# A graph network in one kernel: the third attention's row products in two halves around the turned scan, and residual biases added during the passes

## The chip, the cores and the metric

The kernel runs on one core of one Trainium2 chip, as one program. The metric is the device time of that core in microseconds (us), the median of three runs. The engines are TensorE (PE; its weight loads are PEld), VectorE (DVE), ScalarE (ACT), GpSimd (POOL) and SyncE (SP), which only issues transfers.

## The reference, cut to what matters

There are N = 5000 nodes with 128 features and E = 85000 edges sorted by their target `dst` (the last 5000 in the list before sorting are self loops). Four layers, each `x = x + layer(relu(layernorm(x)))`:

```python
# 0: mean over the incoming edges, then a product
x = x + segment_sum(h[src], dst) / (deg + 1e-6) @ W.T + b
# 1: an edge MLP, its mean, a product, relu
e = relu(concat(h[src], h[dst]) @ W_edge.T)
x = x + relu((segment_sum(e, dst) / deg) @ W_node.T + b_node)
# 2: two graph attentions (16 heads of 8) with elu between them
x = x + gat(elu(gat(h, W1, a_src1, a_dst1) + b1), W2, a_src2, a_dst2) + b2
# 3: dot-product attention (2 heads of 64)
alpha = (q[dst] * k[src]).sum(-1) / 8
a = exp(alpha - segment_max(alpha, dst)[dst])
x = x + segment_sum(a * v[src], dst) / segment_sum(a, dst) + (h @ Wskip + bskip)
```

## The kernel before

**Layout.** X, acc, nodeQ and their like hold all nodes in SBUF: 128 nodes on the partitions, 40 blocks of them along the free axis. The edges are cut into 704 steps of up to 128 edges that all point into one block; eight steps are a group, and there are 88 groups (NG). For each step there are one-hot matrices O (edge to node) and Ot (turned), made in the first pass and kept in DRAM as bf16.

**Stages.** The program is a row of blocks, each with one instruction stream per engine and all engines meeting between blocks: preparation; `norm_phase`; `sum_pass` (layer 0); `sum_to_mlp`; `mlp_pass` (layer 1); `mlp_to_gat`; `softmax_pass("gat")`; `gat_to_gat`; `softmax_pass("gat")`; `gat_to_dot`; `softmax_pass("dot")`, which is called the third attention here; `dot_to_out`.

**A pass** runs one turn per group. GpSimd issues eight indirect gathers a turn (L1000), which bring the rows of the source nodes into GT, a ring of four groups; a place in the ring is free again when VectorE has made the group's values (L1427). SP loads the one-hots (`load_hots`). ScalarE casts them to f32 (L1016 makes Ot32 of the turned ones, two groups deep; L1237 makes O). An order written out by hand sets what each engine does in a turn, with groups that are one or two ahead or behind in it. In the third attention:

- TensorE: the maxima of group p (L1313), the weighted sums of p-2 into psA (L1334), the turning of the logits of p+1 (L1297), the maxima for each edge of p (L1321), the turning back of the scanned maxima of p+1 (L1303, `pe_segT`, into psT), and last the products that bring the query rows of the target nodes to the edges of p+2 (`pe_toedge`, which calls `rows_to_edges`, L1023, eight of 128x128 f32 into psD). A product of f32 is two MATMUL instructions in the trace, so a group of eight is x16. The block numbers come from registers: `loaded` loads eight of them from a table before the products, and eight others (the places of the sums) at the head of the turn.
- VectorE: the product of psD with the keys and its sum over each head for p+1 (L1346, L1355), the running maxima of p (L1378 to L1413), the addition of the sums of p-2 to acc (L1436, L1440), the scan of the turned logits of p+1 (L1362), the difference to the maximum for p (L1418, L1421), three small steps on the turned back maxima of p+1 (`dve_lastmax`, L1370 to L1374), and the values of p (`dve_values`, L1427).
- ScalarE: among others, clearing the places in psA (L1269), and exp of the differences (L1275, the factor that L1427 needs; L1278).

All waits are on semaphores that count groups. One product waits for `turned32` (the cast) and for `prodded` of the group before (psD has been read).

**The stages between the passes** work on 20 units of two blocks, each engine again with an order by hand in which units at several lags alternate (`units`). VectorE's bias additions stand there: L645 in `sum_to_mlp`, L843 (`plus_row`) in `gat_to_gat` and `gat_to_dot`, L928 in `gat_to_dot`; each is followed by an addition to X, a minimum or the like. L862 is one step of elu in `gat_to_gat`. The finished rows of a table are stored by SP (`store_rows`, L525), unit by unit. `dot_to_out` has VectorE divide and add for 20 units (L791 to L980), and when all are done SP stores X in two transfers (L985, L986).

Of the kernel before, what the change touches and what calls it, by code (L numbers as in the profile page):

```python
# [65 lines left out]
def program(nc, x, src, dst, w0, b0, w_edge, w_node, b_node, w1, as1, ad1, b1, w2, as2, ad2, b2,  # L66
# [28 lines left out]
    with ctx:  # L95
# [119 lines left out]
        out_sem = sem("out_stored")  # L215

# [415 lines left out]
        def sum_to_mlp(table):  # L632

            with nc.Block() as block:
                @block.vector
                def _(eng):
                    for unit in units(8):
# [5 lines left out]
                        if n := unit(3):  # L643
                            eng.wait_ge(*made(n.u))
                            eng.tensor_tensor(n.Y, n.ps[:, :, 0:D], bias_row(0), ALU.add).then_inc(biased.sem, 1)  # L645
                            eng.wait_ge(*biased(n.u))
                            eng.tensor_tensor(n.at(X), n.at(X), n.Y, ALU.add).then_inc(xnew.sem, 1)
# [46 lines left out]
            close((degrees, own, denom, mean, cleared, flip, lhs, made, biased, xnew, *norm_counts, flip2, lhs2, made2, kept,  # L694
# [150 lines left out]
        def gat_to_gat(table):  # L845

            with nc.Block() as block:
                @block.vector
                def _(eng):
                    self_shares_1(eng)  # L850
                    self_shares_2(eng)
                    for unit in units(8):
# [7 lines left out]
                        if n := unit(4):  # L860
                            eng.wait_ge(*powered(n.u))
                            eng.tensor_scalar(n.Y2, n.Y2, -1.0, None, ALU.add).then_inc(skipped.sem, 1)  # L862
                            eng.wait_ge(*skipped(n.u))
                            eng.scalar_tensor_tensor(out=n.Y, in0=n.Y, scalar=0.0, in1=n.Y2, op0=ALU.max,
                                                     op1=ALU.add).then_inc(normed.sem, 1)
# [32 lines left out]
            close((own, denom, mean, biased, lowered, powered, skipped, normed, *gat_counts), UNITS)  # L898
            close_stored()

        def gat_to_dot(table):

            with nc.Block() as block:
                @block.vector
                def _(eng):
                    self_shares_1(eng)
                    self_shares_2(eng)
                    for unit in units(8):
                        if n := unit(0):
                            slot_free(eng, n, skipped)  # L910
                            self_and_sums(eng, n)
                            plus_row(eng, n, 3)
                            eng.wait_ge(*biased(n.u))
# [10 lines left out]
                        if n := unit(8):  # L924
# [3 lines left out]
                            eng.tensor_tensor(n.Y, n.ps[:, :, D:2 * D], bias_row(7), ALU.add).then_inc(powered.sem, 1)  # L928
                            eng.wait_ge(*powered(n.u))
                            eng.tensor_tensor(n.at(X), n.at(X), n.Y, ALU.add).then_inc(skipped.sem, 1)  # L930
# [16 lines left out]
                def _(eng):  # L947
                    for unit in units(8):
                        if n := unit(4):
                            slot_free(eng, n, powered)  # L950
                            eng.wait_ge(*normed(n.u))
                            flip_y(eng, n, flip2)
# [8 lines left out]
                def _(eng):  # L961
# [4 lines left out]
            close((own, denom, mean, biased, xnew, cleared, *norm_counts, flip2, lhs2, made2, kept, made3, lowered,  # L966
                   powered, skipped), UNITS)
            close_stored()

        def dot_to_out():  # L970

            with nc.Block() as block:
                @block.vector
                def _(eng):
                    for u in range(UNITS):
                        n = Unit(u)
                        slot_free(eng, n, xnew)
# [5 lines left out]
                def _(eng):  # L983
                    eng.wait_ge(*xnew(UNITS - 1))
                    eng.dma_start(out[0:FULL * P, :].rearrange("(b p) f -> p b f", p=P), X[:, 0:FULL, :]).then_inc(out_sem, 16)  # L985
                    eng.dma_start(out[FULL * P:N, :], X[0:REST, FULL, :]).then_inc(out_sem, 16)  # L986
                    eng.wait_ge(out_sem, 32)
# [30 lines left out]
        def rows_to_edges(eng, p, b):  # L1018

            eng.wait_ge(*turned32(p.g))  # L1020
            eng.wait_ge(*prodded(p.g - 1))
            for j in range(G):
                ins = eng.matmul(psD[:, j, :], Ot32[:, p.q, j, :], at_block(nodeQ, b[j], D), start=True, stop=True)  # L1023
            ins.then_inc(toedge.sem, 1)

        def load_hots(eng, p, rows_free, turned_free):
# [6 lines left out]
            for c in turned_free:  # L1033
# [3 lines left out]
               .then_inc(ring_hotT[p.k].sem, 16)  # L1037

# [18 lines left out]
        def sum_pass(table):  # L1057

            w = D + 1
            with nc.Block() as block:  # L1060
# [37 lines left out]
                def _(eng):  # L1098
                    tables_stored(eng)
# [104 lines left out]
        def softmax_pass(kind, table, h):  # L1204
# [76 lines left out]
            def pe_toedge(eng, p):  # L1281
                if not gat:
                    rows_to_edges(eng, p, loaded(eng, "blocks", blk, p.g, G, NB - 1))
                    return
# [157 lines left out]
            with nc.Block() as block:  # L1442
# [37 lines left out]
                def _(eng):  # L1480
                    def turn(p):
                        if p.has(-2):
                            off = pe_places(eng, p.plus(-2))
# [99 lines left out]
```

## Time and profile before

| | |
|---|---|
| median of 3 runs | 5167.67 us (5164.42 to 5171.92) |
| the profiled execution, its own time | 5178.65 us |
| its span, first to last instruction | 5176.9 us |
| mean granted TensorE clock | 0.686 |
| busy: PE, PEld, DVE | 3180.1, 2813.0, 2733.0 us |
| busy: ACT, POOL | 2152.4, 3365.2 us |

The trace is of the profiled execution. A row of busy time sums an engine's instructions; "idle before" is the time that the engine stood still ahead of an instruction and, behind the arrow, what released it ("issue": nothing that the profile shows, such as loading registers). Matmuls are pipelined, so the time of a group of them includes waiting for the first to come through.

### The profile page before, as it was taken

The page shows a single profiled execution, that of the slowest core. Times are in us where ns is not written, and L with a number is a line of the kernel's source. Part 1 is how long each engine was busy: PE and PEld are TensorE (multiplying, and loading weights), DVE is VectorE, ACT ScalarE, POOL GpSimd, SP SyncE. Part 2 cuts the span into 40 slices and gives each one's busy share as a digit, 9 for nine tenths or more (in the row PEclk, how much of TensorE's full clock was granted, in tenths as well). Part 3 has the DMA queues.
Part 4 walks back from the last instruction along what each step waited for, and adds up shares of the span by engine and source line. Part 5 has one row for each costly group of instructions (what it writes and reads, how often), then busy time and mean ns, then how long its engine had stood idle before and what let it go on. Part 6 is the DMA issues. An engine that isn't in the chain of part 4 may idle for free. (4 is left out here: it accounts for less than half of the span.)

```text
span 5176.9 us, 111400 instructions
## 1 busy us (share of the span) xinstructions
PE 3180.1 (61%) x29524; PEld 2813.0 (54%) x29525; DVE 2733.0 (53%) x6724; ACT 2152.4 (42%) x6586; POOL 3365.2 (65%) x3551
## 2 busy tenths in 40 slices
PE   1555555566666665666666646666665566666664
PEld 0444444455655654565656536566564466666664
DVE  4222222332222225677777767777777666666666
ACT  2222222243333325666666556666664333333332
POOL 1777777557777772777777537777773366666662
PEclk9766666687777777656666656665666777676766
DMA  4333333233333332444444224444441344444442
GB/s 125 106 105 105 105 105 104 80 101 105 105 105 105 105 97 60 115 117 118 117 113 117 78 83 118 117 113 118 117 117 54 111 141 134 133 132 135 134 133 74
DMA packets 331553, 563.97 MB, mean 109 GB/s; under 512 B 79101, under 2 KB 149773, under 8 KB 331438
## 3 DMA queue, kind: packets, MB, share of 16 engines
q0 software_dynamic: 124288, 289.37, 21.2%
q1 hardware_dynamic: 207170, 273.48, 16.3%
q8 instruction: 42, 0.69, 0.1%
q14 instruction: 53, 0.43, 0.0%
HBM read 490.38 MB, written 72.84 MB: 109 GB/s over the span
## 5 line engine op out<-in xcount | busy, mean ns | idle before, releaser
L1000 POOL DMA_INDIRECT GT<-table,srcI x3520 | 3351.0, 952 | 1688.0 <-issue 1055.0
L1334 PE MATMUL psA<-V,O 128*128 128x144 f32 (+1 forms) x4224 | 932.8, 403 | 17.4 <-ACT psA L1269 14.9
L1334 PEld LDWEIGHTS psA<-V,O 128*128 128x128 f32 x4224 | 864.8, 294 | 24.0 <-issue 18.7
L1023 PE MATMUL psD<-nodeQ,Ot 128*128 x2816 | 608.0, 403 | 386.9 <-ACT Ot L1016 298.8
L1023 PEld LDWEIGHTS psD<-nodeQ,Ot 128*128 128x128 f32 x2816 | 561.6, 305 | 416.0 <-issue 416.0
L1055 DVE TENSOR_TENSOR acc<-acc,psA 128x1032 f32 (+1 forms) x176 | 215.1, 1222 | 703.6 <-PE psA L1134 673.9
L1269 ACT COPY psA<-consts 128x1296 f32<-128x1296 f32 (+1 forms) x264 | 318.6, 1207 | 368.0 <-DVE acc L1440 368.0
L1180 DVE TENSOR_TENSOR prod<-psD,GT 128x1024 f32<-128x1024 f32 x88 | 107.7, 1224 | 667.1 <-DMA GT<-table,srcI 667.1
L1046 PE MATMUL psA<-zerob 1*128 1x258 bf16 (+1 forms) x704 | 164.5, 378 | 414.1 <-issue 329.1
L1258 ACT COPY nodeM<-newM 128x16 f32 x1408 | 307.7, 219 | 259.2 <-ACT nodeM L1258 230.3
L1440 DVE TENSOR_TENSOR acc<-acc,psA 128x1296 f32 (+1 forms) x264 | 385.6, 1461 | 55.4 <-PE psA L1334 26.2
L1303 PE MATMUL psT<-ident,seg 128*128 128x128 f32 (+1 forms) x264 | 95.7, 362 | 470.1 <-DVE seg L1362 470.1
L1010 ACT COPY srcI<-srcT 128x8 int32 (+1 forms) x440 | 84.3, 193 | 689.3 <-DMA GT<-table,srcI 682.1
L1263 ACT ACTIVATE resc<-diff 128x16 f32<-128x16 f32 (+1 forms) x264 | 55.9, 212 | 733.5 <-DVE acc L1436 687.6
L1165 ACT ACTIVATE V<-prod 128x1024 f32<-128x1024 f32 x88 | 93.0, 1057 | 616.4 <-DVE prod L1180 616.4
L1321 PEld LDWEIGHTS psS<-newM,Ot 128*128 128x128 bf16 x6336 | 189.3, 99 | 290.8 <-DVE newM L1413 288.9
L1321 PE MATMUL psS<-newM,Ot 128*128 128x16 bf16 (+1 forms) x6336 | 211.3, 174 | 212.8 <-DVE newM L1413 212.5
L1134 PE MATMUL psA<-GT,O 128*128 128x129 f32 x1408 | 329.8, 427 | 0.0
L1134 PEld LDWEIGHTS psA<-GT,O 128*128 128x128 f32 x1408 | 305.9, 329 | 36.6 <-issue 36.6
L1046 PEld LDWEIGHTS psA<-zerob 1*128 1x128 bf16 x704 | 68.7, 118 | 470.5 <-issue 447.6
L1427 DVE TENSOR_TENSOR V<-GT,psA 128x1024 f32<-128x1024 f32 x264 | 320.8, 1215 | 3.7 <-ACT psA L1275 3.4
L1303 PEld LDWEIGHTS psT<-ident,seg 128*128 128x128 f32 (+1 forms) x264 | 43.4, 164 | 492.1 <-DVE seg L1362 323.0
(221 smaller groups left out, 5304.1 us busy)
## 6 DMA issues: line engine op xcount, KB each, us to landing
Ob<-onehots SPq DMA_DIRECT2D x352, 256.0 KB
Ot<-onehots_turned SPq DMA_DIRECT2D x352, 256.0 KB
GT<-table,srcI POOLq DMA_INDIRECT x3520
onehots<-Ob SPq DMA_DIRECT2D x88, 256.0 KB
onehots_turned<-Ot SPq DMA_DIRECT2D x88, 256.0 KB
first<-first_dram SPq DMA_DIRECT2D x176, 64.0 KB
first_dram<-GT SPq DMA_DIRECT2D x18, 384.0 KB, 5.1
table<-GT SPq DMA_DIRECT2D x40, 144.0 KB, 1.9
```

Of the source, the lines that this page charges most:

```text
L1000: eng.indirect_dma_start(out=GT[:, p.k, j, 0:table.shape[1]], out_offset=None, in_=table, in_offset=bass.IndirectOffsetOnAxis(ap=srcI[:, p ...
L1023: ins = eng.matmul(psD[:, j, :], Ot32[:, p.q, j, :], at_block(nodeQ, b[j], D), start=True, stop=True)
L1046: eng.matmul(psA[:, a:a + 2, 0:w], zerob[0:1, 0:P], zerob[0:1, 0:2 * w], start=True, stop=False, skip_group_check=True)
L1055: eng.tensor_tensor(a, a, psA[:, :, 0:w], ALU.add).then_inc(added.sem, 1)
L1134: ins = eng.matmul(to, O[:, p.q, j, :], GT[:, p.k, j, 0:w], start=False, stop=j == G - 1, skip_group_check=True)
L1258: eng.copy(at_block(nodeM, b[j], h), by_step(newM[:, p.q, 0:HG])[:, :, j]).then_inc(noted.sem, 1)
L1269: eng.copy(places, consts[:, 0:1, :].unsqueeze(1).to_broadcast([P, 3, 3, VW])).then_inc(emptied.sem, 1)
L1303: eng.transpose(segR, seg[0:HG, p.q, :], ident[0:HG, 0:HG]).then_inc(segT.sem, 1)
L1321: ins = eng.matmul(edge_max[:, j, :], Ot[:, p.k, j, :], part, start=n == 0, stop=n == 2)
L1334: ins = eng.matmul(flatA[:, bass.ds(off[j], VW)], O[:, p.q, j, :], V[:, p.q, j, 0:VW], start=False, stop=j == G - 1, skip_group_check=True)
L1427: eng.tensor_tensor(v[:, :, :, 0:C], heads(GT[:, p.k, :, f0:f0 + D], h), wide(factors, C), ALU.mult)\
L1440: eng.tensor_tensor(to, to, places, ALU.add).then_inc(added.sem, 1)
```

## The change

Four edits:

- In the third attention TensorE issues the products L1023 as two halves of four, one ahead of the turning back (L1303) and one behind it, and loads their block numbers at the head of the turn. On VectorE `dve_lastmax` moves behind `dve_values`. The attentions of layer 2 keep their order.
- Three biases (b of layer 0, b2, bskip) are added to all of X by `add_to_x`, in four instructions of ten blocks each, at the head of the first sum, the second attention and the third attention, ahead of VectorE's wait for the stored table. L645, L843 in `gat_to_dot`, and L928 go, and the additions to X read psA or its like directly.
- elu's two steps (L862, L864) become one.
- `dot_to_out` stores each unit's rows as soon as they are done, 21 transfers in place of 2.

```diff
--- before
+++ after
@@ -213,6 +213,7 @@
         out_sem = sem("out_stored")
+        leaned = Count(sem("leaned"), 4)
@@ -641,10 +642,9 @@
                         if n := unit(3):
+                            eng.wait_ge(leaned.sem, leaned.base)
                             eng.wait_ge(*made(n.u))
-                            eng.tensor_tensor(n.Y, n.ps[:, :, 0:D], bias_row(0), ALU.add).then_inc(biased.sem, 1)
-                            eng.wait_ge(*biased(n.u))
-                            eng.tensor_tensor(n.at(X), n.at(X), n.Y, ALU.add).then_inc(xnew.sem, 1)
+                            eng.tensor_tensor(n.at(X), n.ps[:, :, 0:D], n.at(X), ALU.add).then_inc(xnew.sem, 1)
                         if n := unit(3):
@@ -859,10 +859,8 @@
                             eng.wait_ge(*powered(n.u))
-                            eng.tensor_scalar(n.Y2, n.Y2, -1.0, None, ALU.add).then_inc(skipped.sem, 1)
-                            eng.wait_ge(*skipped(n.u))
-                            eng.scalar_tensor_tensor(out=n.Y, in0=n.Y, scalar=0.0, in1=n.Y2, op0=ALU.max,
-                                                     op1=ALU.add).then_inc(normed.sem, 1)
+                            eng.scalar_tensor_tensor(out=n.Y, in0=n.Y2, scalar=-1.0, in1=n.Y, op0=ALU.add,
+                                                     op1=ALU.max).then_inc(normed.sem, 1)
                         if n := unit(8):
@@ -907,10 +905,10 @@
                         if n := unit(0):
-                            slot_free(eng, n, skipped)
+                            slot_free(eng, n, flip2)
                             self_and_sums(eng, n)
-                            plus_row(eng, n, 3)
-                            eng.wait_ge(*biased(n.u))
+                            eng.wait_ge(leaned.sem, leaned.base)
+                            eng.wait_ge(*mean(n.u))
                             eng.tensor_tensor(n.at(X), n.at(X), n.Y, ALU.add).then_inc(xnew.sem, 1)
@@ -925,9 +923,7 @@
                                                      op0=ALU.mult, op1=ALU.add).then_inc(lowered.sem, 1)
-                            eng.tensor_tensor(n.Y, n.ps[:, :, D:2 * D], bias_row(7), ALU.add).then_inc(powered.sem, 1)
-                            eng.wait_ge(*powered(n.u))
-                            eng.tensor_tensor(n.at(X), n.at(X), n.Y, ALU.add).then_inc(skipped.sem, 1)
+                            eng.tensor_tensor(n.at(X), n.ps[:, :, D:2 * D], n.at(X), ALU.add).then_inc(skipped.sem, 1)
@@ -947,7 +943,8 @@
                         if n := unit(4):
-                            slot_free(eng, n, powered)
+                            slot_free(eng, n, lowered)
+                            slot_free(eng, n, skipped)
                             eng.wait_ge(*normed(n.u))
@@ -974,6 +970,8 @@
                         n = Unit(u)
+                        if not u:
+                            eng.wait_ge(leaned.sem, leaned.base)
                         slot_free(eng, n, xnew)
@@ -981,10 +979,14 @@
                 def _(eng):
+                    whole_rows = out[0:FULL * P, :].rearrange("(b p) f -> p b f", p=P)
+                    for u in range(UNITS - 1):
+                        eng.wait_ge(*xnew(u))
+                        eng.dma_start(whole_rows[:, u * H:(u + 1) * H, :], X[:, u * H:(u + 1) * H, :]).then_inc(out_sem, 16)
                     eng.wait_ge(*xnew(UNITS - 1))
-                    eng.dma_start(out[0:FULL * P, :].rearrange("(b p) f -> p b f", p=P), X[:, 0:FULL, :]).then_inc(out_sem, 16)
+                    eng.dma_start(whole_rows[:, (UNITS - 1) * H:FULL, :], X[:, (UNITS - 1) * H:FULL, :]).then_inc(out_sem, 16)
                     eng.dma_start(out[FULL * P:N, :], X[0:REST, FULL, :]).then_inc(out_sem, 16)
-                    eng.wait_ge(out_sem, 32)
+                    eng.wait_ge(out_sem, 16 * (UNITS + 1))
             close((own, denom, mean, xnew), UNITS)
@@ -1015,13 +1017,15 @@
-        def rows_to_edges(eng, p, b):
-            eng.wait_ge(*turned32(p.g))
-            eng.wait_ge(*prodded(p.g - 1))
-            for j in range(G):
+        def rows_to_edges(eng, p, b, half=None):
+            if not half:
+                eng.wait_ge(*turned32(p.g))
+                eng.wait_ge(*prodded(p.g - 1))
+            for j in range(G) if half is None else range(half * G // 2, (half + 1) * G // 2):
                 ins = eng.matmul(psD[:, j, :], Ot32[:, p.q, j, :], at_block(nodeQ, b[j], D), start=True, stop=True)
-            ins.then_inc(toedge.sem, 1)
+            if half != 0:
+                ins.then_inc(toedge.sem, 1)
@@ -1035,6 +1039,13 @@
                .then_inc(ring_hotT[p.k].sem, 16)
+        def add_to_x(eng, c):
+            for q in range(4):
+                part = X[:, q * NB // 4:(q + 1) * NB // 4, :]
+                eng.tensor_tensor(part, part, bias[:, c:c + 1, :].to_broadcast([P, NB // 4, D]), ALU.add).then_inc(leaned.sem, 1)
+            leaned.close(1)
@@ -1096,6 +1107,7 @@
                 def _(eng):
+                    add_to_x(eng, 0)
                     tables_stored(eng)
@@ -1201,7 +1213,7 @@
-        def softmax_pass(kind, table, h):
+        def softmax_pass(kind, table, h, to_x=None):
             gat = kind == "gat"
@@ -1279,9 +1291,6 @@
             def pe_toedge(eng, p):
-                if not gat:
-                    rows_to_edges(eng, p, loaded(eng, "blocks", blk, p.g, G, NB - 1))
-                    return
                 eng.wait_ge(*staged(p.g))
@@ -1481,6 +1490,8 @@
                             off = pe_places(eng, p.plus(-2))
+                        if not gat and p.has(2):
+                            b = loaded(eng, "blocks", blk, p.g + 2, G, NB - 1)
                         if p.has(0):
@@ -1489,14 +1500,21 @@
                             pe_maxedge(eng, p)
+                        if not gat and p.has(2):
+                            rows_to_edges(eng, p.plus(2), b, 0)
                         if p.has(1):
...
                         if p.has(2):
-                            pe_toedge(eng, p.plus(2))
+                            if gat:
+                                pe_toedge(eng, p.plus(2))
+                            else:
+                                rows_to_edges(eng, p.plus(2), b, 1)
                     sweep(eng, NG, turn, early=2, late=2)
...
                 def _(eng):
+                    if to_x is not None:
+                        add_to_x(eng, to_x)
                     tables_stored(eng)
@@ -1527,10 +1545,12 @@
                             dve_below(eng, p)
-                        if p.has(1):
+                        if gat and p.has(1):
                             dve_lastmax(eng, p.plus(1))
...
                             dve_values(eng, p)
+                        if not gat and p.has(1):
+                            dve_lastmax(eng, p.plus(1))
                     sweep(eng, NG, turn, early=2, late=2)
@@ -1552,9 +1572,9 @@
         gat_to_gat(T3)
-        softmax_pass("gat", T3, HEADS1)
+        softmax_pass("gat", T3, HEADS1, to_x=3)
         gat_to_dot(T4)
-        softmax_pass("dot", T4, HEADS3)
+        softmax_pass("dot", T4, HEADS3, to_x=7)
         dot_to_out()
...
```

## Rows read from the trace of the kernel before

**Rows 1.** Windows: us, busy us (x) of PE, PEld, DVE, ACT, POOL, clock, DMA share, GB/s.

```profile
4080.00:4290.00 210.00, 131.10 (x1379) 121.31 (x1379) 127.72 (x318) 66.26 (x172) 148.24 (x157) 0.74 0.48 146
4290.00:5110.00 820.00, 551.05 (x5659) 513.64 (x5659) 527.83 (x1316) 268.25 (x689) 516.96 (x546) 0.72 0.44 132
```

**Rows 2.** The line L1346: durations ns min/median/max, first and last start, idle before.

```profile
L1346 DVE TENSOR_TENSOR prod<-psD,GT x88: 1223/1225/1225, 4088.9 to 5114.6; 128x1024 f32<-128x1024 f32 x88
...
  PE psD L1023: 241.5, 85
```

**Rows 3.** Timeline of one turn: start us, us, engine line op [idle before].

```profile
4601.93 1.04 ACT L1016 CAST Ot<-Ot 128x1024 f32<-128x1024 bf16 x1
...
4604.67 1.22 DVE L1346 TENSOR_TENSOR prod<-psD,GT 128x1024 f32<-128x1024 f32 x1 [2.56 <-PE psD L1023]
...
4608.74 0.76 PE L1321 MATMUL psS<-newM,Ot 128*128 128x2 bf16 x24 [1.26 <-DVE newM L1413]
...
4610.94 0.40 DVE L1362 TENSOR_TENSOR_SCAN seg<-first,psT 16x128 f32<-16x128 f32 x1
...
4611.49 0.26 PE L1303 MATMUL psT<-ident,seg 16*128 16x16 f32 x1 [1.99 <-DVE seg L1362]
4611.92 0.18 DVE L1370 TENSOR_TENSOR lastmax<-psT,lastT 128x16 f32<-128x16 f32 x1 [0.30 <-PE psT L1303]
...
4612.21 0.18 ACT L1275 ACTIVATE psA<-below 128x16 f32<-128x16 f32 x1
...
4612.43 1.22 DVE L1427 TENSOR_TENSOR V<-GT,psA 128x1024 f32<-128x1024 f32 x1
...
4612.74 3.78 PE L1023 MATMUL psD<-nodeQ,Ot 128*128 x16 [1.00 <-issue]
...
4616.31 0.83 PE L1313 MATMUL psS<-lastmax,Ob 128*128 128x3 bf16 x24
```

**Rows 4.** As rows 2 for L1180, which starts a turn in the second layer's pass.

```profile
L1180 DVE TENSOR_TENSOR prod<-psD,GT x88: 1223/1225/1226, 1089.0 to 1960.0; 128x1024 f32<-128x1024 f32 x88
...
  DMA GT<-table,srcI: 667.1, 88
```

**Rows 5.** Timeline of GpSimd at the start of the third attention.

```profile
4077.41 0.95 POOL L1000 DMA_INDIRECT GT<-table,srcI  x1 [141.72 <-ACT srcI L1010]
...
4087.44 0.95 POOL L1000 DMA_INDIRECT GT<-table,srcI  x1 [0.30 <-issue]
```

**Rows 6.** Timeline: the sums of two turns that follow each other.

```profile
4605.09 2.05 PE L1334 MATMUL psA<-V,O 128*128 128x130 f32 x16
...
4617.10 3.83 PE L1334 MATMUL psA<-V,O 128*128 128x130 f32 x16
```

**Rows 7.** Groups by shape: out<-in, shapes, count | busy us, mean ns | idle before.

```profile
L843 DVE TENSOR_TENSOR O<-O,bias 128x256 f32<-128x256 f32 x40 | 17.0, 424 | 1.4
L862 DVE TENSOR_SCALAR V<-V 128x256 f32<-128x256 f32 x20 | 5.7, 285 | 0.0
L645 DVE TENSOR_TENSOR O<-psA,bias 128x256 f32<-128x256 f32 x12 | 5.0, 418 | 2.1 <-PE psA L520 2.1
```

**Rows 8.** Timeline of ScalarE in `sum_to_mlp`: its one step of a unit with idle time before.

```profile
1031.61 0.37 ACT L568 COPY Ob<-psD 128x256 f32<-128x256 f32 x1 [0.34 <-PE psD L515]
```

**Rows 9.** Timeline: the first sums of the first pass, the first L1346.

```profile
132.87 1.04 PE L1046 MATMUL psA<-zerob 1*128 1x258 bf16 x4 [8.12 <-issue]
...
4088.94 1.22 DVE L1346 TENSOR_TENSOR prod<-psD,GT 128x1024 f32<-128x1024 f32 x1 [12.09 <-DMA GT<-table,srcI]
```

**Rows 10.** Timeline: the first table's stores and their end; the output's store.

```profile
95.16 23.02 SPq L525 DMA_DIRECT2D table<-O  x19
116.16 1.63 ACT L560 ACTIVATE O<-X,st 128x128 f32<-128x128 f32 x4
119.90 0.29 DVE L1100 COPY psS<-iota 128x128 f32<-128x128 f32 x1 [1.14 <-DMA table<-O]
...
5166.13 0.41 SPq L985 DMA_DIRECT2D out<-X  x1
```

More of the change, by code:

```diff
@@ L693, in _ @@
                         store_rows(eng, n, table, n.R, kept)
-            close((degrees, own, denom, mean, cleared, flip, lhs, made, biased, xnew, *norm_counts, flip2, lhs2, made2, kept,
+            close((degrees, own, denom, mean, cleared, flip, lhs, made, xnew, *norm_counts, flip2, lhs2, made2, kept,
                    noted_rows), UNITS)
@@ L897, in gat_to_gat @@
             close((whole, whole_exp), 1)
-            close((own, denom, mean, biased, lowered, powered, skipped, normed, *gat_counts), UNITS)
+            close((own, denom, mean, biased, lowered, powered, normed, *gat_counts), UNITS)
             close_stored()
@@ L965, in gat_to_dot @@
             close((whole, whole_exp), 1)
-            close((own, denom, mean, biased, xnew, cleared, *norm_counts, flip2, lhs2, made2, kept, made3, lowered,
-                   powered, skipped), UNITS)
+            close((own, denom, mean, xnew, cleared, *norm_counts, flip2, lhs2, made2, kept, made3, lowered, skipped), UNITS)
             close_stored()
```

## The prediction

> **What bounds the kernel now.** I read the busy times by stage first, then the third attention's products line, then one of its turns in order of time, and last the four stages between passes. In the third attention no engine is full: VectorE is busy 528 us of an 820 us stretch, TensorE 551, GpSimd 517, the granted TensorE clock is 0.72 and the DMA engines are at 0.44 [rows 1]. So a loop of waits sets the pace. The line that starts a turn on VectorE (L1346) runs 88 times from 4088.9 to 5114.6 us, so a turn takes 1025.7 / 87 = 11.79 us, and VectorE stands 241.5 us before it, 2.8 us a turn, for TensorE's psD [rows 2].
>
> One turn shows the loop [rows 3]. Counted from L1346's start at 4604.67: the maxima per edge (L1321) are done at 4.83, the scan L1362 ends at 6.67, its transposition L1303 runs at 6.82 to 7.08, then TensorE is idle 1.00 us on "issue" (the eight registers of the blocks are loaded there), and the eight products L1023 take 3.78 us, to 11.85. The next L1346 follows at once. VectorE does its last steps (L1370, L1427) beside this. Between L1321's end at 4609.50 and L1303 at 4611.49 TensorE has nothing to do: 1.99 us. The cast of the turned one-hots that the products read (L1016) ended at 4602.97, and L1346 has read psD by 4605.89, so all that the products need is there before that gap.
>
> **The floor.** In the second layer's pass L1180 runs 88 times from 1089.0 to 1960.0 us, 10.01 us a turn, and always waits for the gathered rows [rows 4]. That is GpSimd issuing eight gathers in a row. In the third attention, where rows are twice as wide, the first eight go out from 4077.41 to 4087.44, so 10.03 us a turn is the least here too [rows 5].
>
> **The third attention, step by step.** Half of L1023 moves into the idle 1.99 us. It waits for the cast and for L1346 only, both long done, so it starts at about 4.85. The eight products run at 3.41 us once started (3.78 less some 0.37 for the first to come through, an estimate from the row), so a half is 1.7 to 1.9: it ends at 6.6 to 6.75, as the scan ends at 6.67. The transposition behind it on TensorE is late by 0 to 0.1. The register loads go to the turn's head, so the second half follows at 7.08 and ends near 8.9: psD is ready 2.9 us earlier. What is late next? VectorE. Its order becomes L1418, L1421, L1427, then L1370 and its two followers. L1427 waits for ScalarE's factor (L1275, 7.54 to 7.72), so it stays at 7.76 to 8.98; the three small steps that stood ahead of it, 0.21 each, now come behind, to 9.6. L1346 could start at 9.65. (The reorder thus costs 0.6 in this chain; in the old order it would be 9.05. It pays only if the transposition is late.) Both are under 10.03, so gathers become the bound, and the reorder is hidden by them; if that cover were gone it would cost 0.6 x 88 = 53 us.
>
> TensorE's own round must fit as well. With the slower sums (3.83 [rows 6]): maxima 0.8, sums 3.8, two transposes 0.6, L1321 0.8, two halves 3.6, in sum 9.6. The loads now stand ahead of L1313, sixteen registers instead of eight; the first eight stood there already, and L1313 shows no idle time behind L1023 [rows 3], so those are hidden. The added eight cost 1.00 if bare, and they stand behind a shorter stretch of products. Bounds: 0 and 1.0 a turn, so 9.6 to 10.6 where the sums are slow, and 7.8 to 8.8 where they take 2.05 [rows 6]. I take little of it, because the sequencer has the whole second half to run ahead in: 10.10 a turn on average instead of 10.03. DMA traffic per turn is 132 GB/s x 11.79, at 10.1 us it is 154 GB/s; the highest that this pass shows is 146 at a share of 0.48 [rows 1], which is far from full, so nothing for it. Sum: 87 x (11.79 - 10.10) = **147 us less**; bounds 87 x (11.79 - 10.03) = 153 and, at 10.6, 104.
>
> **Between the passes** VectorE paces, with hardly any gaps. Into the third attention, each of 20 units loses L843 and L928, 0.42 and (of the same shape as L645, psA plus a bias) 0.42 [rows 7], with 0.03 between instructions: 0.9 x 20 = 18; the last units wait for TensorE, so **16**. Between the attentions L862 goes, 0.285 and 0.03: **6**. After the first sum L645 goes, 0.42 + 0.03, 9 us; but ScalarE there has only 0.34 idle in a unit, in one place [rows 8] and becomes the bound, so 20 x 0.3, rounded down: **5**. The changed waits for free slots are for earlier or equal events: nothing.
>
> **The biases** cost three times four additions of 10 blocks. L843 takes 0.424 for 2 blocks [rows 7], so 2.1 each at most, 8.5 us a pass. VectorE sits idle 12.09 us at the head of the third attention, waiting for the first gather [rows 9]; the second attention starts in the same way. In the first sum the one-hots come at most 8.5 us later; TensorE starts its sums there at 132.9 after 8.12 idle us [rows 9], and the pass is paced by gathers: nothing. SP and ScalarE get no new instruction in these passes.
>
> A rule of the Trainium skill speaks against this (SBUF, State Buffer, "Who interferes with whom"): a VectorE instruction with both inputs in SBUF contends with a GpSimd one that reads SBUF, and the one that comes second waits. No row here shows such an addition of this length beside a gather; by the rule up to the whole 8.5 us a pass would come back, 25 in all, and the total would be 5011. It is a rival below.
>
> **The output** leaves in 20 pieces as units end. Now 10.8 us lie between its issue at 5166.13 [rows 10] and the span's end, 5176.9. The first table is stored in such pieces by SP, 19 of them in 23.02 us, 1.28 each, and was all there 2.1 us after the last part was computed (L560 ends at 117.8, VectorE, which waits for the stores, goes on at 119.90 [rows 10]). SP's issue takes 0.41 and fits into a unit. So 10.8 - 2.1 - 0.4 for the second issue at the end: **8** less. The Trainium skill (DMA: Bandwidth & Descriptors, "Anatomy of one DMA") puts some 2.0 us fixed on each DMA, mostly its completion; if pieces paid that in turn, 20 of them would take 40 us, end some 15 us after VectorE, and the total would be near 5000. The stores of [rows 10] overlap, so I go by them.
>
> **Sum:** 147 + 16 + 6 + 5 + 8 = 182. The profiled execution took 5178.65 us, so 4996.65 by its own time; it is 11.0 above the median of the runs, 5167.67, and I forecast **5167.67 - 182 = 4986**.
>
> **The rivals.**
> A. Gathers bound the third attention, as above: 4968 to 5000. For it: [rows 4, 5]. Chance 0.76.
> B. TensorE's round is the bound: loads bare and slow sums, 10.4 to 10.7 a turn, 95 to 121 saved there: 5012 to 5038. For it: a granted clock of 0.72 [rows 1] is more than half of the time at 1.2 of 2.4 GHz, and in single turns the sums took 3.83 [rows 6]. Against it: the first eight loads are hidden now, and no row speaks for a lower clock when TensorE idles less. Chance 0.12.
> C. The additions hold up the gathers at the head of three passes, up to 25 us: 4987 to 5011. VectorE's additions would start at 4076.85 (4088.94 less 12.09), the gathers at 4077.41 [rows 5, 9], so they meet. Against it: in the third attention a gather takes 516.96 / 546 = 0.95 us beside VectorE's steps on SBUF [rows 1], the same as in [rows 5], where VectorE is idle. Chance 0.05.
> D. DMA at its end at 146 GB/s: 132 x 11.79 / 146 = 10.66 a turn, 98 saved: 5035. Chance 0.02.
> E. The change does not do what it says: half 0 is held back (its cast or the registers come after the scan), both halves run after it as now, and only the 1.00 of loading goes: 87 saved at most, less 0.6 x 88 for the reorder, so 34, and 35 in the other stages: 5099. Chance 0.02.
> F. Slower: half 0 holds the transposition. It stands ahead of L1303 on TensorE, with the last maxima, L1313 and the next turn behind it. If the cast L1016 comes y us after the scan, a turn is 6.67 + y + 1.9 + 0.3 + 1.9, then the place of L1346: 10.8 + y. It is slower than before once the turn passes 11.79 + 35/87 = 12.2, so y over 1.4; the cast would have to be about 10 us later than in [rows 3]. With y = 2.4 a turn is 13.2, 87 x 1.41 = 123 more, less the 35: 5256. Chance 0.02, and 0.01 for no change.
>
> **How the numbers follow.** A to E are faster: 0.97; F is slower 0.02. No change is within 0.2% of 5167.67, some 10 us, about what a measurement can tell: 0.01. The range holds A, C, D and most of B: 4966 to 5040.
>
> **What would show it.** In the changed profile L1346 should be 10.0 to 10.2 apart and wait for "DMA GT<-table" in place of psD; L1023 in two groups around L1303, the second with no "issue" ahead of it; L1427 ahead of L1370; GpSimd's "DVE V L1427" wait almost gone; the table of stages shorter by 16, 6 and 5; the span ending some 3 us after the last L980. L1346 still waiting for psD at 10.4 or more means B; first gathers more than 1.3 apart while the additions run means C; gathered rows late with gathers that themselves wait means D; L1023's first half after L1303 means E.

## The result and the profile after

The changed kernel takes 4995.16 us (median of 4 runs, 4994.31 to 4995.68) against 5167.77 of the kernel before (4 runs, 5164.42 to 5171.92): ratio 0.9665, 95% interval 0.9649 to 0.9682, or 172.6 us less. The forecast was 4986, with a range of 4966 to 5040.

The third attention first: windows of its start and of the stretch behind it (columns as in [rows 1]), then the line that starts a turn, L1355 now.

```profile
4055.00:4265.00 210.00, 150.81 (x1580) 136.94 (x1581) 147.56 (x368) 77.06 (x201) 159.14 (x168) 0.71 0.52 158
4265.00:4930.00 665.00, 503.30 (x5437) 456.51 (x5435) 505.17 (x1256) 255.92 (x658) 503.57 (x531) 0.77 0.52 157
```

```profile
L1355 DVE TENSOR_TENSOR prod<-psD,GT x88: 1223/1225/1226, 4064.1 to 4937.6; 128x1024 f32<-128x1024 f32 x88
...
  DMA GT<-table,srcI: 57.5, 88
```

A turn takes 873.5 / 87 = 10.04 us, where it took 11.79 [rows 2], and all 88 waits are for gathered rows now. The DMA engines move 157 GB/s at a share of 0.52, more than the 146 that was the highest before [rows 1]. One turn, in order of time:

```profile
4500.32 2.06 PE L1026 MATMUL psD<-nodeQ,Ot 128*128 x8
...
4501.94 0.40 DVE L1371 TENSOR_TENSOR_SCAN seg<-first,psT 16x128 f32<-16x128 f32 x1
...
4502.48 0.26 PE L1312 MATMUL psT<-ident,seg 16*128 16x16 f32 x1
...
4502.67 1.74 PE L1026 MATMUL psD<-nodeQ,Ot 128*128 x8
...
4503.42 1.22 DVE L1436 TENSOR_TENSOR V<-GT,psA 128x1024 f32<-128x1024 f32 x1 [0.81 <-ACT psA L1287]
...
4504.56 0.17 DVE L1379 TENSOR_TENSOR lastmax<-psT,lastT 128x16 f32<-128x16 f32 x1
...
4505.55 1.23 DVE L1355 TENSOR_TENSOR prod<-psD,GT 128x1024 f32<-128x1024 f32 x1 [0.38 <-DMA GT<-table,srcI]
```

Against [rows 3]: half 0 fills the gap ahead of the turning back (L1312), which runs 0.14 us after the scan, as before; half 1 follows without the 1.00 us of "issue"; psD is ready at 4504.41, 1.14 us before L1355 starts. VectorE waits 0.81 us for the factor, and does the small steps (L1379) behind the values.

Where the rest went, by the starts of the same lines in both traces:

| from, to (line numbers of before) | before | after | difference |
|---|---|---|---|
| L640 first to L1180 first (`sum_to_mlp`) | 78.8 | 78.4 | -0.4 |
| L802 (2967.10; 2963.44) to the second attention's first L1343 (3056.43; 3048.15), `gat_to_gat` | 89.3 | 84.7 | -4.6 |
| L1343 last to L1346 first (`gat_to_dot`) | 150.4 | 134.8 | -15.6 |
| L1346 first to last (third attention) | 1025.7 | 873.5 | -152.2 |
| L1346 last to the end of the span | 62.3 | 55.4 | -6.9 |

The spans differ by 183.9 us (5176.9 and 4993.0); the 4.2 us that the table lacks lie mainly between the first L1180 and the first L802, where the changed kernel takes 5.2 us less with the same code. The section on why the prediction was right or wrong comes back to this.

### The profile page after: what moved, and what is told of

The parts are those of the page before. It is cut to its first block and busy times, and to the rows that moved or that the text cites. A ratio compares the mean times of both kernels' runs of the same rounds, so it can differ in the third digit from the quotient of the medians.

```text
span 4993.0 us, 111471 instructions
## 1 busy us (share of the span) xinstructions
PE 3144.0 (63%) x29524; PEld 2769.8 (55%) x29525; DVE 2722.5 (55%) x6656; ACT 2152.1 (43%) x6586; POOL 3365.4 (67%) x3551
## 5 line engine op out<-in xcount | busy, mean ns | idle before, releaser
L1343 PE MATMUL psA<-V,O 128*128 128x144 f32 (+1 forms) x4224 | 986.9, 421 | 17.4 <-ACT psA L1281 15.0
L1343 PEld LDWEIGHTS psA<-V,O 128*128 128x128 f32 x4224 | 916.5, 311 | 24.1 <-issue 18.4
L1026 PE MATMUL psD<-nodeQ,Ot 128*128 x2816 | 535.8, 359 | 290.8 <-ACT Ot L1018 290.8
L1026 PEld LDWEIGHTS psD<-nodeQ,Ot 128*128 128x128 f32 x2816 | 477.2, 261 | 315.1 <-issue 311.8
L1322 PE MATMUL psS<-lastmax,Ob 128*128 128x17 bf16 (+1 forms) x6336 | 207.8, 173 | 262.7 <-DVE lastmax L1383 229.5
L1322 PEld LDWEIGHTS psS<-lastmax,Ob 128*128 128x128 bf16 x6336 | 189.0, 103 | 292.5 <-issue 292.3
L1312 PE MATMUL psT<-ident,seg 128*128 128x128 f32 (+1 forms) x264 | 96.5, 366 | 365.2 <-DVE seg L1371 364.5
```

Source lines behind the costliest of these rows:

```text
L1322: ins = eng.matmul(maxima[:, j, :], Ob[:, p.k, j, :], part, start=n == 0, stop=n == 2)
L1343: ins = eng.matmul(flatA[:, bass.ds(off[j], VW)], O[:, p.q, j, :], V[:, p.q, j, 0:VW], start=False, stop=j == G - 1, skip_group_check=True)
```

## The experiments

Twelve kernels were run. `third_only`, `split_no_reorder`, `loads_only` and `old_first_bias` shared one chip (before: 5168.22 us); the three with seven gathers and `loads_at_half` another (before: 5180.41 us); the last four a third (before: 6829.85 us).

**The third attention's parts.** `third_only` is the kernel before with the edit of that pass alone. `split_no_reorder` leaves VectorE's order as it was. `loads_only` moves nothing but the register loads:

```diff
 # TensorE's turn, loads_only
                         if p.has(-2):
                             off = pe_places(eng, p.plus(-2))
+                        if not gat and p.has(2):
+                            b = loaded(eng, "blocks", blk, p.g + 2, G, NB - 1)
...
                         if p.has(2):
-                            pe_toedge(eng, p.plus(2))
+                                rows_to_edges(eng, p.plus(2), b)
```

> The kernel before with the third attention's edit alone (two halves, register loads at the turn's head, the last maxima behind the values); everything else as before. Theory (the third attention carries nearly all, and gathers bound it afterwards): turns of 10.04 us from one L1346 to the next, as in the changed kernel, so 152 us less by the profiles, and 5167.8 - 141 to 152 = 5016 to 5027 as a median; VectorE waits for gathered rows. Rival (the other stages' edits also free something in the pass): turns above 10.1 and a saving under 140.

> As third_only, but VectorE keeps its old order (the last maxima ahead of the values). Theory (gathers are the bound, VectorE's order is hidden by them): the same time as third_only within 2 us, turns of 10.04, and the wait for gathered rows ahead of L1346 longer by some 0.6 a turn. Rival (the transposition comes late behind half 0 and VectorE needs the new order): turns of 10.3 or more and a wait on psT ahead of the first of the last maxima.

> The kernel before with one thing alone: in the third attention the eight block registers are loaded at the head of TensorE's turn and the eight products stay together behind the turning back. Theory: exactly the 1.00 us of issue ahead of L1023 goes, turns of 10.8 us, 87 us less. Rival (sixteen loads at the turn's head come out bare ahead of L1313): under 60 us less, with an issue time ahead of L1313. Second rival (L1023 still waits): no change.

Measured, against 5168.22: 5022.33 us (ratio 0.9716, 0.9700 to 0.9732), 5019.65 (0.9713, 0.9697 to 0.9729) and 5039.46 (0.9748, 0.9732 to 0.9764), that is 145.9, 148.6 and 128.8 us less. The line that starts a turn, in `third_only`:

```profile
L1348 DVE TENSOR_TENSOR prod<-psD,GT x88: 1218/1225/1226, 4080.6 to 4956.4; 128x1024 f32<-128x1024 f32 x88
...
  DMA GT<-table,srcI: 66.6, 86
```

in `split_no_reorder`:

```profile
L1348 DVE TENSOR_TENSOR prod<-psD,GT x88: 1223/1225/1226, 4080.6 to 4955.9; 128x1024 f32<-128x1024 f32 x88
...
  DMA GT<-table,srcI: 107.4, 88
```

in `loads_only`:

```profile
L1346 DVE TENSOR_TENSOR prod<-psD,GT x88: 1223/1225/1226, 4082.7 to 4977.3; 128x1024 f32<-128x1024 f32 x88
...
  PE psD L1023: 103.8, 84
```

Turns are 10.07, 10.06 and 10.28 us. So the pass's own edit carries 146 of the 173 us, and the new order on VectorE nothing: without it the wait for gathered rows is longer by 40.8 / 88 = 0.46 us a turn and the time is the same within 3 us.

`loads_only` is the surprise: all theories had 87 us or less for it, and it gives 129, or 1.51 us a turn, where only some 1.0 of issue could go. Its turns show the rest (timeline, the products of three turns):

```profile
4500.32 3.77 PE L1023 MATMUL psD<-nodeQ,Ot 128*128 x16
...
4511.51 2.87 PE L1023 MATMUL psD<-nodeQ,Ot 128*128 x16
...
4521.56 2.71 PE L1023 MATMUL psD<-nodeQ,Ot 128*128 x16 [0.17 <-issue]
```

The products themselves are shorter in many turns. Grouped over the steady part of the pass, first the kernel before (4200 to 5100), then `loads_only` (4200 to 4965; count | busy us, mean ns | idle us ahead of them):

```profile
L1023 PE MATMUL psD<-nodeQ,Ot 128*128 x1212 | 281.8, 426 | 78.5 <-issue 78.5
```

```profile
L1023 PE MATMUL psD<-nodeQ,Ot 128*128 x1187 | 223.8, 365 | 9.6 <-issue 2.7
```

16 instructions a turn make 281.8 x 16 / 1212 = 3.72 us before and 3.02 now: 0.70 less. The idle time ahead of them goes from 78.5 x 16 / 1212 = 1.04 us to 0.13: 0.91 less. Together that is 1.61 us, which covers the saving: the turns in the middle of the pass are 1.59 apart (11.86 and 10.27), those of the whole pass 1.51. The instructions are the same; the granted clock is not (windows over the products of one turn, columns as in [rows 1]), before:

```profile
4517.69:4521.47 3.78, 3.78 (x23) 3.72 (x24) 0.90 (x1) 2.07 (x6) 2.66 (x3) 0.50 0.60 152
```

in `loads_only`:

```profile
4511.51:4514.38 2.87, 2.86 (x16) 2.57 (x16) 1.73 (x4) 2.87 (x9) 2.08 (x3) 0.68 0.34 94
```

0.50 is 1.2 GHz throughout; 0.68 is part of the time at 2.4. The clock is not higher over the whole pass, though (0.70 over 4265 to 4930, where the kernel before has 0.73 in the same window). Its low stretch fell on other work, the weighted sums (L1334, the products with the values; grouped, 4265 to 4930), before and in `loads_only`:

```profile
L1334 PE MATMUL psA<-V,O 128*128 128x130 f32 x898 | 143.2, 323 | 0.0
```

```profile
L1334 PE MATMUL psA<-V,O 128*128 128x130 f32 x1031 | 215.2, 391 | 0.0
```

Two windows over these sums, a turn before ([rows 6]) and one in `loads_only`:

```profile
4605.09:4607.14 2.05, 2.05 (x21) 1.86 (x18) 2.02 (x3) 0.00 (x0) 1.44 (x3) 1.00 0.40 130
```

```profile
4515.35:4519.18 3.83, 3.83 (x20) 3.70 (x18) 2.98 (x11) 0.00 (x0) 2.85 (x3) 0.50 0.63 211
```

The kernel before has sums at either clock ([rows 6]); on average they go from 143.2 x 16 / 898 = 2.55 us a turn to 3.34, 0.79 longer. This fits into what TensorE idled for VectorE: its waits for the scan (`seg`) and for newM fall from 159.4 us over 56 turns to 113.3 over 64, 1.1 us a turn. So the low clock moved in part from products that VectorE waited for to products that had room. That the missing microsecond of idle is what moved it is argued from the order of the turn, not shown. The Trainium skill (TensorE: Matmul & The Clock Gate, "HAM oscillation") describes a clock that falls in waits between groups of matmuls; which group then runs slowly is what the trace adds.

**The floor and what lies under it.** Seven of a group's eight gathers are issued in the third attention; the eighth step computes on zeros, which VectorE sets in a block of its own ahead of the pass, so that part of the sums is missing from the output.

```diff
+        for c in ring_rows:
+            c.by = 16 * (G - 1)
         softmax_pass("dot", T4, HEADS3)
...
-                for j in range(G):
+                for j in range(ring_rows[0].by // 16):
                     eng.indirect_dma_start(
```

> The kernel before, but in the third attention only seven of the eight gathers of a group are issued; the eighth step of every group computes on zeros that are set once ahead of the pass. Theory (before the change the gathers are not the bound, the loop of VectorE and TensorE is): turns of 11.8 us as before, within 0.2. Rival (gathers already share the pace): turns shorter by up to 1.25.

> The changed kernel with seven gathers of eight in the third attention, as in before_seven. Theory (the gathers are the bound after the change, VectorE's chain is next): the gathers' floor falls to 7 x 1.254 = 8.8, turns of 10.04 - 0.65 to 0.76 (the wait for gathered rows per turn) = 9.3 to 9.4, and up to 9.65 by the prediction's sum. Rival (TensorE's round is next, 9.6 to 10.6): turns above 9.7 and a wait for psD.

> after_seven with VectorE's old order, the last maxima ahead of the values. Theory (the new order costs 0.5 to 0.6 us in VectorE's chain, hidden so far by the gathers): turns of 8.8 to 9.1, shorter than after_seven by 0.3 to 0.6. Rival (the new order is worth something, since the turning back comes late behind half 0): turns longer than after_seven.

Measured: 5181.46 (ratio 1.0001, 0.9991 to 1.0011), 4962.59 (0.9578, 0.9559 to 0.9597), 4914.66 us (0.9486, 0.9467 to 0.9505). `before_seven`, then `after_seven`, then `after_seven_old_order`:

```profile
L1346 DVE TENSOR_TENSOR prod<-psD,GT x88: 1224/1225/1227, 4091.4 to 5118.0; 128x1024 f32<-128x1024 f32 x88
...
  PE psD L1023: 249.7, 87
```

```profile
L1355 DVE TENSOR_TENSOR prod<-psD,GT x88: 1216/1225/1226, 4073.3 to 4903.4; 128x1024 f32<-128x1024 f32 x88
...
  PE psD L1026: 1.1, 1
```

```profile
L1355 DVE TENSOR_TENSOR prod<-psD,GT x88: 1211/1218/1225, 4073.1 to 4860.1; 128x1024 f32<-128x1024 f32 x88
...
  PE psD L1026: 0.5, 2
```

Turns of 11.80, 9.54 and 9.05 us. Fewer gathers bring the kernel before nothing and the changed one half a microsecond a turn: the bound has moved from the loop to the gathers. Under it lies the chain of VectorE's steps, with its wait for ScalarE's factor, and neither of the two waits for psD. The new order costs 0.49 us in that chain, which the gathers hide.

**Loads right ahead of half 0** (`loads_at_half`, the changed kernel with the load moved):

```diff
-                        if not gat and p.has(2):
-                            b = loaded(eng, "blocks", blk, p.g + 2, G, NB - 1)
...
                         if not gat and p.has(2):
+                            b = loaded(eng, "blocks", blk, p.g + 2, G, NB - 1)
                             rows_to_edges(eng, p.plus(2), b, 0)
```

> The changed kernel with the eight block registers loaded right ahead of half 0 in place of the turn's head: 1.0 us of loading and a half of 1.1 to 1.9 us then stand in TensorE's idle 2 us ahead of the turning back. Theory (gathers are the bound and VectorE's new order waits for the turning back only 1.9 us later): the turning back comes 0.3 to 0.9 late, the same time within 3 us, 4995. Rival (a late turning back or second half sets the turn): turns of 10.2 to 10.9, 14 to 75 us slower.

Measured: 5006.12 us, ratio 0.9662 (0.9645 to 0.9678); the changed kernel's 0.9665, from the other chip, lies in that interval. Half 0 and the turning back, then L1355's first and last start and its waits:

```profile
4502.32 1.15 PE L1026 MATMUL psD<-nodeQ,Ot 128*128 x8 [0.63 <-issue]
...
4502.76 0.40 DVE L1371 TENSOR_TENSOR_SCAN seg<-first,psT 16x128 f32<-16x128 f32 x1
...
4503.40 0.23 PE L1312 MATMUL psT<-ident,seg 16*128 16x16 f32 x1
```

```profile
L1355 DVE TENSOR_TENSOR prod<-psD,GT x88: 1218/1225/1226, 4074.2 to 4950.0; 128x1024 f32<-128x1024 f32 x88
...
  DMA GT<-table,srcI: 49.7, 70
  PE psD L1026: 7.8, 15
```

In this turn the turning back comes 0.24 us after the scan instead of 0.14; over the 76 turns in the middle of the pass it is 0.43 on average and at most 1.23 (0.15 in the changed kernel). Fifteen of the 88 turns wait for psD, but the turn is 10.07. Where the loads stand hardly matters once the gathers bound the pass.

**The first bias** (`old_first_bias`: the changed kernel with L645 back and no additions in the first sum).

> The changed kernel with the first bias as before: VectorE adds it to psA's result in sum_to_mlp, and nothing is added to X during the first sum. Theory (ScalarE's own loop sets sum_to_mlp's pace, the unit was 2.82 us before and after, and the additions cost the first gathers 1.6 us): 0 to 1 us longer in sum_to_mlp, 1 to 2 us less ahead of it, in sum 0 to 2 us FASTER than the changed kernel, 4993 to 4995. Rival (VectorE paced that stage, as the prediction said): 5 us slower, 5000.

Measured: 4993.90 us (4992.68 to 4996.45), 1.3 us under the changed kernel and inside its own spread, so unclear as a time, but not the 5 us more of the rival. The changed kernel's trace says why: ScalarE's same step in two units of `sum_to_mlp`, and VectorE's wait between them.

```profile
1030.28 0.37 ACT L569 COPY Ob<-psA 128x256 f32<-128x256 f32 x1 [0.34 <-PE psA L516]
...
1032.79 0.17 DVE L553 RECIPROCAL st<-st 128x2 f32<-128x2 f32 x1 [0.40 <-ACT st L549]
...
1033.10 0.37 ACT L569 COPY Ob<-psD 128x256 f32<-128x256 f32 x1 [0.34 <-PE psD L516]
```

A unit takes 2.82 us with 0.45 us less for VectorE to do, as it did before (1031.61 to 1034.43 from one such wait of L568 to the next) and as it does in this run's own trace. The 0.34 idle of ScalarE is a wait inside its own loop (it normalises, TensorE turns, ScalarE copies), not room.

**The additions, the stores and a combination**, on the third chip. `no_adds_in_passes` leaves the three biases out of the output.

> The changed kernel once more, on the same chip as the three runs beside it, to compare them with. Expected: 0.9665 of the kernel before, turns of 10.04 us in the third attention.

> The changed kernel without its three additions of a bias to all of X (the bias of layer 0, b2 and bskip are left out of the output). Theory (VectorE's four additions hold up the gathers that run beside them, by 1.6, 1.5 and 0.7 us at the heads of the three passes, and each pass that gathers bound is later by that): 3.8 us less than the changed kernel. Rival 1 (the additions lie beside the gathers for nothing, as the prediction's sum had it): 0 us. Rival 2 (a gather waits for all of the additions): 17 us less.

> The changed kernel with the output stored in two transfers after the last unit, as before. Theory (a store in pieces overlaps with VectorE, and what remains is 2 us from the last piece's issue to its end, in place of 10.8): 8.8 us more than the changed kernel. Rival (pieces pay their fixed cost in turn): no difference or less.

> The changed kernel with the first bias as before (old_first_bias) and VectorE's old order (split_no_reorder): what the runs so far leave of the change as useful. Theory: 1 to 2 us less than the changed kernel for the first gathers, and 0 to 1 for the order, since gathers bound the pass and the order only comes out at its end. Rival (the two parts that are undone were worth something): 0 to 5 us more.

Measured there: 6863.42 (ratio 1.0053, 1.0040 to 1.0066), 6864.95 (1.0053, 1.0040 to 1.0066), 6875.36 (1.0065, 1.0052 to 1.0078), and 6729.48 us for the combination (0.9851, 0.9837 to 0.9866). On this chip the kernel before takes 32% longer, and the changed kernel is 0.5% slower than it: inside the 2% that count as the same here, but beyond the interval. The single instructions of the timeline take no longer than on the other chips; what grows is the time between them. TensorE, then VectorE, in the changed kernel:

```profile
6104.26 0.70 PE L1330 MATMUL psS<-newM,Ot 128*128 128x2 bf16 x20 [1.26 <-DVE newM L1422]
...
6105.41 0.17 PE L1330 MATMUL psS<-newM,Ot 128*128 128x2 bf16 x1 [0.45 <-issue]
...
6108.23 0.16 PE L1330 MATMUL psS<-newM,Ot 128*128 128x2 bf16 x1 [1.24 <-issue]
...
6109.71 1.38 DVE L1449 TENSOR_TENSOR acc<-acc,psA 128x1170 f32 x1 [4.56 <-remote]
```

Twenty of 24 small products run in 0.70 us, and the last four take 4 us with no wait that the profile knows. VectorE stands still in the same stretch, 4.56 us, released by no engine of the core, while GpSimd issues its gathers every 1.25 us as ever. The turn is (6804.1 - 5398.4) / 87 = 16.16 us, and 14.60 in the combination; the passes that the change does not touch are longer as well. What holds up the engines there stays open, and so does how the combination saves 1.56 us a turn: in this pass it differs from the changed kernel in VectorE's order alone, but there is no trace of the kernel before from this chip, and no run of the old order by itself. As times, these runs therefore do not settle the 3.8 us of the additions (1.5 us more without them, where 3.8 less was expected), nor the stores (11.9 us more, 8.8 expected, with runs that overlap). The heads and ends of the traces are undisturbed and do tell. Gathers at the head of the first pass, the changed kernel (`after_again`), then without the additions:

```profile
120.77 2.22 POOL L1002 DMA_INDIRECT GT<-table,srcI  x1 [60.38 <-DMA table<-O]
123.29 1.10 POOL L1002 DMA_INDIRECT GT<-table,srcI  x1 [0.30 <-issue]
...
131.10 0.95 POOL L1002 DMA_INDIRECT GT<-table,srcI  x1 [0.30 <-issue]
```

```profile
119.98 0.94 POOL L1002 DMA_INDIRECT GT<-table,srcI  x1 [60.38 <-DMA table<-O]
...
128.72 0.94 POOL L1002 DMA_INDIRECT GT<-table,srcI  x1 [0.30 <-issue]
```

From the first to the eighth gather 10.33 us against 8.74: the additions cost the gathers 1.59 us. The output's end, with pieces (`after_again`, span 6859.5), then with two transfers (`two_stores`, span 6872.9):

```profile
6857.45 0.35 SPq L987 DMA_DIRECT2D out<-X  x1
```

```profile
6862.18 0.41 SPq L983 DMA_DIRECT2D out<-X  x1
```

2.05 us against 10.7 from the issue to the end of the span: 8.7 us for the pieces.

## Why the prediction was right or wrong

**The third attention** went by the forecast's mechanism: loop before, gathers after, psD early, VectorE next. The sum had 147 us; the profiles give 152.2, since the turn came to 10.04, not 10.10, and `third_only` as a time 145.9. Of the 0.07 added for the eight more loads at the turn's head at most 0.04 was there (10.07 in `third_only`), and `loads_at_half`, without them at the head, is at 10.07 too. The chain of 9.65 was 9.54, the old order's 9.05 was 9.05.

**The price of the loads alone** was mis-sized. In the case that only the 1.00 us of loading went, 87 us was called the most; `loads_only` measured 129, because TensorE's low clock moved off these products in part (0.70 us a turn). The 1.7 to 1.9 us for a half were an average that few halves have: a half takes 1.15 or some 2.06 us, as the clock is, and 1.41 on average in the changed kernel. Of the 146 us, then, the split itself adds only 17 over the moved loads; the floor of the gathers cuts off the rest.

**Between the passes.** Into the third attention 16 was 15.6. Between the attentions 6 was 4.6, as the gathers that end this stretch are held up by 1.5 (below). Between kernels with the same code these stretches differ by up to 2.2 us (148.2 to 150.4 for `gat_to_dot`), so tenths count for nothing here. **`sum_to_mlp` failed**: 5 forecast, 0.4 measured. The step was reading ScalarE's 0.34 of idle time as room; it was part of the loop that already set the pace.

**The biases** were costed at nothing. VectorE's time is hidden, as forecast (5.7 us a pass, under the 8.5 allowed), but the gathers beside it are not: 1.6 us in the first pass. In the changed kernel's third attention the additions start 1.1 us ahead of the gathers:

```profile
4050.74 5.70 DVE L1047 TENSOR_TENSOR X<-X,bias 128x1280 f32<-128x1280 f32 x4 [0.32 <-PEq L901]
4051.81 1.24 POOL L1002 DMA_INDIRECT GT<-table,srcI  x1 [125.04 <-ACT srcI L1012]
4053.36 1.09 POOL L1002 DMA_INDIRECT GT<-table,srcI  x1 [0.30 <-issue]
...
4061.31 0.94 POOL L1002 DMA_INDIRECT GT<-table,srcI  x1 [0.30 <-issue]
```

Seven steps take 9.50 us here instead of the 8.77 that seven spacings of 10.03 / 8 make [rows 5], 0.7 more; the second attention's head (3035.34 to 3045.61) has 1.5 more. That is rival C at 3.8 us in sum at the three heads, not 25; what of it reaches the end, no time shows. The lengths of the gathers give the mechanism. The four additions start 1.40 us apart and last 1.49 each:

```profile
L1047 DVE TENSOR_TENSOR X<-X,bias x12: 1484/1486/1493, 120.2 to 4055.0; 128x1280 f32<-128x1280 f32 x12
```

The first gather starts when the running addition has 1.40, 1.35 and 0.42 us left in the three passes, and takes 1.27, 1.22 and 0.29 us more than its 0.945. The gathers after it start 1.40 us apart, as the additions do, until these are over. So every gather waits for the end of the addition that runs, as the rule says that the forecast cited (the Trainium skill, SBUF — State Buffer, "Who interferes with whom"). But one gather then gets through per addition, so that each costs 0.15 us over the 1.25 that a gather takes anyway. The forecast priced the rule as if all of the 8.5 us were lost.

**The output** gave 8.8 (10.8 to 2.0) for 8, and the pieces overlap. The Trainium skill (DMA: Bandwidth & Descriptors, "Anatomy of one DMA") has some 2.0 us as the fixed part of one DMA. That section is on transfers issued by GpSimd; for these, issued by SP, the 2.0 us that remain at the end agree with it.

**The sum met the spans by luck.** Its terms make 182 and the spans differ by 183.9, but the medians by 172.6. The terms as the runs have them are 145.9 (`third_only`), 15.6, 4.6, 0.4 and 8.8, less the 1.6 at the head of the first pass: 173.7, close to the 172.6. So the 9 us by which 4986 fell short of 4995 are terms that were too large: `sum_to_mlp` by 4.6, and the biases, which held up gathers by 1.6, 1.5 and 0.7 (the last two lie inside the stretches of 4.6 and 15.6). The spans hid this, because the profiled execution of the kernel before was slow, 11.0 us above its median, while that of the changed kernel lies at its median (4994.77). `third_only` shows where most of this lay: its span is 156.0 us below that of before, but only 147.7 of them come after the start of the first L1346 (4088.9; its L1348 4080.6); the other 8.3 lie in stages whose code is the same in both. The profiled 5178.65 us would be an ordinary time on the second chip (5169.72 to 5182.43); on which chip it was taken is not on record.

**The rivals.** B (TensorE's round), D (DMA at 146 GB/s), E and F did not occur on the first two chips: psD is early, 157 GB/s flow, and the turning back is on time. C was there at a seventh of its price. On the third chip the change was slower, by a mechanism that none of them named.

## What to carry to other kernels

Where two engines hand a turn to each other, register loads behind a wait are bare time. Moving them ahead of it was worth half as much again as their length here (1.51 us a turn for 1.0), since TensorE's low clock then fell more on other matmuls; that it could go the other way is a guess. Before work is split or reordered further, the next floor should be priced: here the moved loads alone would have given 129 of the 146 us. An idle stretch of an engine is room only if what it waits for does not depend on its own last output. And before a difference of two profiles is taken as a gain, stages that both kernels share should be compared: here they alone differed by 8.3 us.

## What was not expected of the hardware

A gather's issue on GpSimd takes 0.94 us alone. Beside VectorE additions with both inputs in SBUF it ends only after the addition that runs: 1.10 us in step with them, and 2.22, 2.17 and 1.24 for the one that comes first. On one of three chips the same kernel took 6830 us in place of 5168, with instructions on TensorE 0.7 to 1.4 us apart for no recorded reason, and there the change turned from 3.4% faster to 0.5% slower, while the version with the old order and the old first bias was 1.5% faster. Its gain on the other chips was not measured.
